# First attention, second score pass: the far tile of each pair of heads first, and each head's band right behind its score product

## What is computed

```python
scores = jnp.einsum('bhid,bhjd->bhij', q, k) * scale
diag = i - j
in_band = causal & (diag < MAX_BIAS_LENGTH)          # 128
bias = jnp.where(in_band, learnable_bias[:, jnp.clip(diag, 0, MAX_BIAS_LENGTH - 1)], 0.0)
scores = jnp.where(causal, scores + bias, -jnp.inf)
m = jnp.maximum(jnp.max(scores, axis=-1), off)
p = jnp.exp(scores - m[..., None])
denom = jnp.sum(p, axis=-1) + jnp.exp(off - m)
out = jnp.einsum('bhij,bhjd->bhid', p, v) / denom[..., None]
```

## Time and profile before

| | before |
|---|---|
| median of 3 runs | 1211.83 us (1206.76 to 1213.01) |
| the profiled execution's own time | 1214.93 us |
| its span, first to last instruction | 1212.6 us |
| busy: TensorE / VectorE / ScalarE / GpSimd | 84% / 67% / 48% / 26% |
| mean granted clock of TensorE | 0.947 |
| second look of the 8 groups | 191.96 to 493 us |

### The profile page before, as it was taken

How to read it: one execution, slowest core, us unless ns; L and a number is a source line. 1 busy time by engine, 2 the same in 40 slices (tenths; PEclk the granted TensorE clock), 3 DMA queues, 4 the chain that set the end, 5 groups by cost and what they waited for, 6 DMA issues and landing times.

```text
span 1212.6 us, 21037 instructions
## 1 busy us (share of the span) xinstructions
PE 1015.3 (84%) x7768; PEld 671.0 (55%) x7768; DVE 812.0 (67%) x1979; ACT 584.5 (48%) x1231; POOL 319.0 (26%) x212
## 2 busy tenths in 40 slices
PE   1798768999999998699787678898988988889697
PEld 1587612333333333478565556676666766667575
DVE  6745887787777771479778546666666666666654
ACT  1533224556656567254444235545445555454264
POOL 4010230000000000000033105555545464555344
PEclk9999857999999999899989699999999999999998
DMA  7010254312332100110121000000000000000001
GB/s 165 1 70 3 87 132 66 60 36 47 62 67 52 27 11 1 36 53 18 70 70 35 1 1 1 2 1 1 2 1 1 1 2 1 2 1 1 1 1 35
DMA packets 24038, 37.12 MB, mean 31 GB/s; under 512 B 2992, under 2 KB 21040, under 8 KB 22160
## 3 DMA queue, kind: packets, MB, share of 16 engines
q1 hardware_dynamic: 23936, 35.78, 12.8%
HBM read 31.31 MB, written 4.27 MB: 29 GB/s over the span
## 4 chain that ended last, share of the span: by engine, by line
PE 62%; DVE 22%; issue 8%; ACT 5%; DMA 1%; SPq 1%; POOL 1%; DVEq 0%; POOLq 0%; ACTq 0%
PE bank L923 18%; PE pair L1207 6%; PE bank L1251 6%; PE bank L1057 6%; PE bank L1086 5%; PE bank L1047 4%; PE bank L989 4%; DVE mx L1586 4%; PE bank L1239 3%; PE bank L1072 3%; ACT PT L825 2%; DVE PT L1619 2%; PE bank L953 2%; DVE bank L1462 2%; DVE hL L1386 1%
## 5 line engine op out<-in xcount | busy, mean ns | idle before, releaser
L705 POOL TENSOR_SCALAR P<-P,rec 128x1024 f32<-128x1024 f32 (+7 forms) x128 | 220.4, 1724 | 228.3 <-DVE rec L1611 228.3
L825 ACT ACTIVATE PT<-bank 128x512 f32<-128x512 f32 (+3 forms) x384 | 165.7, 493 | 103.7 <-PE bank L1072 87.7
L1462 DVE CUSTOM_DVE_ANT_0 bank<-bank,stripS 128x512 f32<-128x512 f32 (+3 forms) x256 | 148.9, 606 | 54.6 <-PE bank L1047 51.7
L1047 PE MATMUL bank<-KT,QT 96*128 96x512 bf16 (+3 forms) x384 | 126.5, 365 | 26.8 <-DVE MX L1462 11.9
L1239 PE MATMUL bank<-ident,P 128*128 128x128 f32 x576 | 99.0, 281 | 45.9 <-DVE PT L1619 33.7
L1057 PE MATMUL bank<-QT,KT 128*128 128x512 bf16 (+3 forms) x384 | 112.9, 336 | 12.9 <-ACT PT L825 11.0
L1207 PE MATMUL pair<-KH,QH 128*128 128x512 f16 (+3 forms) x576 | 115.4, 328 | 5.6 <-ACT P L872 4.2
L1251 PE MATMUL bank<-PT,VH 128*128 128x128 f16 x1728 | 117.2, 219 | 0.1
L872 ACT ACTIVATE P<-pair,nm 128x1024 f32<-128x1024 f32 (+7 forms) x128 | 95.6, 747 | 43.8 <-DVE nm L1590 43.8
L1251 PEld LDWEIGHTS bank<-PT,VH 128*128 128x128 f16 x1728 | 107.1, 98 | 2.8 <-DVE PT L1619 0.2
L1619 DVE TENSOR_TENSOR PT<-bank,PT 128x384 f16<-128x384 f32 (+1 forms) x192 | 99.7, 547 | 11.8 <-ACT PT L713 11.8
(11 more groups left out here) (178 smaller groups left out, 1920.0 us busy)
## 6 DMA issues: line engine op xcount, KB each, us to landing
stripS<-band_rows SPq DMA_DIRECT2D x32, 128.0 KB, 2.1
KT<-qk_dram SPq DMA_DIRECT2D x21, 192.0 KB
qk_dram<-parts SPq DMA_DIRECT2D x12, 256.0 KB, 2.4
cprow<-cp SPq DMA_DIRECT2D x9, 256.0 KB, 11.1
stripT<-seq_dram SPq DMA_DIRECT2D x24, 88.0 KB, 9.1
q_raw<-w_gu SPq DMA_DIRECT2D x4, 512.0 KB, 4.0
w_raw<-w_q SPq DMA_DIRECT2D x2, 1024.0 KB, 5.9
w_raw<-w_dense SPq DMA_DIRECT2D x2, 1024.0 KB, 5.4
```

Of the source, the lines that this page charges most:

```text
L705: pool.tensor_scalar(rows, rows, rec1[:, m % 4:m % 4 + 1], None, ALU.mult).then_inc(s["pn"], 1)
L825: act.activation(PT[:, jb % 2, h, o:o + ni], bank[2 + i2 % 3][:, 0:ni], ACT.Exp).then_inc(s["s2_exp"], 1)
L1047: pe.matmul(ring_bank(use)[:, 0:nj], queries(g)[0:ROWS, h, P * ib:P * (ib + 1)], KT3[0:ROWS, g % 3, h, j0:j0 + nj], start=True, stop=True) ...
L1462: dve.tensor_tensor_reduce(out, out, stripS[:, h, HALF - nj:HALF], 1.0, LOWEST, ALU.add, ALU.max, mx).then_inc(s["s1_max"], 1)
```

## The change

In a step of blocks 0 to 3 the far tiles (c = 1) of the two heads come first and the near ones behind the values; each `look2_band` follows directly behind its own `look2`, where before the two bands of a pair stood together, behind a tile of the first look. `at_s2` numbers the tiles in the new order, and ScalarE's loop runs over them in that order. The wait for the maxima rows moves to the tile that is now first, that for the strips to the band that is now first. No instruction is added or taken away, and no size changes.

```diff
-            return N2 * g + first2[jb] + 2 * len(tiles2(jb)) * (h // 2) + 2 * c + h % 2
+            return N2 * g + first2[jb] + 2 * len(tiles2(jb)) * (h // 2) + 2 * (len(tiles2(jb)) - 1 - c) + h % 2
...
-                        for c, (b, i0, ni) in enumerate(tiles2(jb)):
+                        for c, (b, i0, ni) in reversed(list(enumerate(tiles2(jb)))):
...
-                if jb == 0 and h % 2 == 0 and c == 0:
+                if jb == 0 and h % 2 == 0 and c == 1:
                     pe.wait_ge(m_in[h // 2], 32 * (g + 1))
...
-                if jb == 0 and h == 0:
+                if jb == 0 and h == 0 and c == 0:
                     pe.wait_ge(strip_t[g % 2], 48 * (g // 2 + 1))
...
-                        look2(g, jb, h, 0)
-                        look2(g, jb, h + 1, 0)
+                        last = len(tiles2(jb)) - 1
+                        look2(g, jb, h, last)
+                        look2_band(g, jb, h, last)
+                        look2(g, jb, h + 1, last)
+                        look2_band(g, jb, h + 1, last)
                         for i in ahead[:1]:
                             look1(i)
-                        look2_band(g, jb, h, 0)
-                        look2_band(g, jb, h + 1, 0)
                         values_at(g, st)
-                        if len(tiles2(jb)) > 1:
-                            look2(g, jb, h, 1)
+                        if last:
+                            look2(g, jb, h, 0)
+                            look2_band(g, jb, h, 0)
                         for i in ahead[1:2]:
                             look1(i)
-                        if len(tiles2(jb)) > 1:
-                            look2(g, jb, h + 1, 1)
-                            look2_band(g, jb, h, 1)
-                            look2_band(g, jb, h + 1, 1)
+                        if last:
+                            look2(g, jb, h + 1, 0)
+                            look2_band(g, jb, h + 1, 0)
                         for i in ahead[2:]:
                             look1(i)
                         transposition(turn(g, st))
```

## The result

The changed kernel takes 1256.71 us in the median of 4 runs (1246.52 to 1258.08), against 1212.42 us (4 runs) for the kernel before: the ratio is 1.0351, with a 95% interval of 1.0283 to 1.0419. It is slower by some 43 us. The forecast was 1240, with a range from 1224 to 1256. Put on the median of 1211.83 that the forecast started from, the ratio gives 1254.4, just inside the range; the measured median itself lies 0.7 us above it. The sign and the mechanism were right; the forecast of 27.8 us was two thirds of what came.

What follows compares the result with a forecast made beforehand. TensorE was taken to bound the kernel, busy for 84% of the span. Groups 0 to 5 add 24.0 us, group 6 3.8, group 7 0: +27.8, so 1242.7 from the profiled 1214.9, or 1240 for the median; range 1224 to 1256.

Steps and rivals of the forecast that it cites:

- visits: Runs of narrow TensorE instructions (bands, values) between full-width ones; 48 in place of 18 in a full group, 6.1 us gross.
- The price of a visit: TensorE's holes going into and out of narrow instructions, 0.204 us together, taken to hold for each new run.
- The same bank: Rival: a band directly behind its own product waits 0.08 us more, 23 us in all, 1255 to 1263; chance 0.12.
- What is given back: Waits in a full group that the new order removes: 2.1 us of the 6.1 gross, leaving 4.0 us lost.
- steps 5 to 7: Within a group, one wait for an exponential in each (0.26, 0.20, 0.44 us) goes with the new order.
- Steps 0 and 1: First steps of a group: exponentials start 0.4 us earlier; together 4.9 us in place of 5.0.
- step 13: Late in a group: TensorE waits for VectorE's maxima (1.14 us idle), and the step's added narrow runs vanish in that time.
- group 7: Last group, without first look: 23 more narrow runs cost 4.7 us, all given back by waits for exponentials; net 0.
- One sum among the rivals: Rival that waits give back twice as much (4.2 us): a group loses 1.9, 1212 + 15 = 1227; chance 0.13.
- The clock: Dips of TensorE's granted clock cost 1.0 us each; one or two more or fewer, 1 to 3 us either way.

Runs made afterwards that it cites:

- bands_follow_only: Kernel before with near tiles still first, but each band moved directly behind its own product; 1251.44 us, ratio 1.0303.
- one_run: Kernel before with far tiles first, bands paired; in blocks 0 to 2 near products, then their bands and values in one narrow run; 1213.17 us, ratio 0.9993.
- split_bands: Kernel before with one first-look tile moved from ahead of the two bands to between them; 1229.78 us, ratio 1.0116.
- follow_late_only: Kernel before with each band directly behind its product in blocks 4 to 7 only; 1237.47 us, ratio 1.0188.

## Why the forecast was right or wrong

**The bound and the mechanism: right.** The loop is set by TensorE, and the change adds visits. The kernels with counts of visits in between have periods in between: 38.33 and 38.45 us for 18 visits, 38.97 for 23, 40.3 to 40.8 for 31 to 35, 42.33 for 45, 42.88 for 48. The tiles' order is not the cause; with near tiles first the loop is as long (342.96 against 342.58 and 343.35 us). A price of a visit that holds everywhere does not follow: 17 visits in blocks 0 to 3 add 2.01 us to a period, 13 in blocks 4 to 7 add 2.49, and 23 in the last group 0.1.

**The price of a visit: a little low.** 0.204 was taken from runs of eight bands, or of bands and values. A run of four bands has 0.10 to 0.11 ahead and 0.11 to 0.12 behind, together 0.22 to 0.23; and a values run without bands ahead is 0.02 longer from its start to the next one's (0.78 against 0.76 for 384 columns). The forecast period was 42.3 against 42.89. Over seven groups the 0.56 is 4 us.

**The same bank: no cost.** The upper bound of 0.08 more for a band behind its own product did not come: 0.11 ahead of it, and 0.11 elsewhere too.

**What is given back: right in sum, wrong in cause.** 2.1 of 6.1 us was forecast; with visits at 0.22 to 0.23 it is 2.0 to 2.3. But the reason given for steps 5 to 7, "in the new order the tile three before is a whole run of values back, so these waits go", is not needed: bands_follow_only loses the same waits with the near tile first, so the added visits fill them. By itself the order takes away the one of step 7 (one_run) and next to nothing of those in steps 5 and 6, whose length is 2.71 and 2.30 there against 2.71 and 2.36. Steps 0 and 1 took 4.93 at the full clock (326.59 to 331.52; forecast 4.9), step 13 still waits for VectorE's maxima, and group 7 is unchanged, all as laid out. One sum among the rivals was off: 1.9 us in each of seven groups are 13 and not 15.

**The clock: the term that was too small.** The forecast let the dips vary by "1 to 3 us either way". The loop is 40.05 us longer. Of this six full groups at 4.56 are 27.4; group 6 is 3.9 (41.21 less about half of the 3.06 us dip, against 35.78); group 7 is 0.1. That leaves 8.7 us to the dips, as four of about 3.06 against three of 1.0 or a little more would give. I had priced a dip by its cost in the kernel before, and had not thought of its length as something that changes with the order of instructions. Both the number and the lengths differ between these kernels.

**Outside the loop.** Span less loop is 913.7 us against 910.1, at the same instructions. Over the profiles of all kernels it lies between 903.7 and 913.7 (907.1 and 911.3 for two more with 48 visits, 903.7 for one with 18), so 3.6 us are within the scatter of single executions, and no cause is claimed. In sum: 27.8 forecast; 31.4 from visits, 8.7 from dips, 3.6 outside, 43.7 in the profiles.

**The range: some luck.** The chance of 0.67 went to 18 to 36 us above the kernel before, and the result of some 43 lies above that. Over 36 us only the same-bank rival was expected, with 0.12, and its mechanism is not what happened. The top of the range stood at 1256 partly for that rival, and the clock's loss, which no case had at this size, ended just inside it.

## What to carry to other kernels

Count the changes between full-width matmuls and matmuls on column groups, and put all narrow work of a step in one run. Each added run costs 0.22 us of TensorE here. How much of it waits hide depends on where it stands: about a third over a whole period, nearly half in blocks 0 to 3 (17 visits, 2.01 us), and nearly all in the last group, where TensorE waits for ScalarE. An idle time that disappears from an engine's row is no gain by itself; ask whether something longer stands in its place. And where a kernel runs near TensorE's limit, compare periods at the same granted clock first, then count the dips and their lengths as a loss of their own.

## What the runs showed of the hardware that was not expected

The length of a dip of the granted clock went with the order of instructions. In the kernel before all three dips that begin in the loop were 3.4 us long, in split_bands one was 3.4 and one 6.8. In the changed kernel four in each of two profiles were 10.2 us, in bands_follow_only 10.2 and more, in follow_late_only up to 10.2. Pairing the bands in steps 14 and 15 alone brought nearly all of them back to 3.4. The long ones began in steps 13 and 14 of a group, and ran into step 0 of the next. Only the changed kernel was profiled twice, so for the others this is one execution each; and outside the loop the kernel before has dips of 10.2 us and more as well.

Where a dip begins is alike in all ten profiles. In groups 0 to 5 there are 35, and each begins in step 13 or 14, 0.4 to 2.4 us behind the start of the product that ends TensorE's longest wait of the group, the one for VectorE in step 13 (1.06 to 1.44 us). That product, in the kernel before 1.2 us ahead of the dip at 304.6, and in the changed one 1.7 us ahead of the dip at 366.1:

```profile
303.46 0.39 PE L1047 MATMUL bank<-KT,QT 96*128 96x512 bf16 x1 [1.14 <-DVE MX L1462]
```

```profile
364.33 0.39 PE L1047 MATMUL bank<-KT,QT 96*128 96x512 bf16 x1 [1.06 <-DVE MX L1463]
```

The wait is as long where no dip follows, as in three of these six groups of the kernel before, and much the same ahead of short dips and long ones. Whether the dips go when it goes was not tried. What TensorE did behind it differed little: a dozen short matmuls apart or together. Why one dip lasts three times as long stays open.
